# Shared expert of a routed feed-forward layer: units of 128 inner rows by 512 tokens in place of 256 by 256, and a down product in every unit

## What is computed

```python
x = x + xattn(layernorm(x), ctx, ...)          # 32 x 112 tokens of 256, 8 heads of 64
x = x + ffn(layernorm(x), ...)
# ffn, on n = layernorm(x), 3584 tokens:
out = routed(n)                                # 2 of 8 experts for each token, weighted
hs = (n @ Ws1) * silu(n @ Ws3)                 # shared expert: 256 -> 512 inner rows
out = out + hs @ Ws2                           # 512 -> 256
```

## Time and profile before

| what | value |
|---|---|
| median of 3 runs | 1096.32 us (1096.11 to 1097.06) |
| the profiled execution's own time | 1097.37 us |
| its span | 1095.3 us |
| mean granted TensorE clock | 0.985 of full |
| PE busy | 1061.2 us of the span |
| DVE busy | 743.3 us |
| ACT busy | 694.3 us |
| POOL busy | 705.3 us |

### The profile page before, as it was taken

One profiled execution on the slowest core, in us unless ns is written; L12 is line 12 of the kernel. 1 busy time (PEld: TensorE's weight loads), 2 busy tenths in 40 slices (PEclk: granted clock), 3 DMA queues, 4 the chain that ended last, 5 costly groups with the idle time before them and its releaser, 6 DMA issues. The chain is left out here.

```text
span 1095.3 us, 25507 instructions
## 1 busy us (share of the span) xinstructions
PE 1061.2 (97%) x7342; PEld 929.1 (85%) x7342; DVE 743.3 (68%) x1940; ACT 694.3 (63%) x1649; POOL 705.3 (64%) x658
## 2 busy tenths in 40 slices
PE   6999999999999999999999899999999999999996
PEld 4788888888888888888887799999888888888886
DVE  5788888888888888888888676656443333433332
ACT  6888888888888888888886554332334343343442
POOL 4988889888988888898887556555033223332233
PEclk9999999999999999999998999889999999999998
DMA  8014431442144214421532295223473354333861
GB/s 247 17 41 131 139 103 37 139 139 94 45 139 139 86 53 139 139 78 62 178 103 94 77 304 185 81 76 127 147 217 56 58 137 87 56 56 62 269 176 15
DMA packets 83985, 124.06 MB, mean 113 GB/s; under 512 B 7904, under 2 KB 48080, under 8 KB 83920
## 3 DMA queue, kind: packets, MB, share of 16 engines
q1 hardware_dynamic: 63664, 99.86, 28.0%
q0 software_dynamic: 11760, 15.15, 7.7%
q10 hardware_dynamic: 8496, 8.22, 2.6%
HBM read 74.44 MB, written 49.68 MB: 113 GB/s over the span
## 5 line engine op out<-in xcount | busy, mean ns | idle before, releaser
L559 POOL TENSOR_TENSOR probs<-probs,first_rows 112x750 f32<-112x750 f32 x128 | 184.0, 1438 | 66.1 <-DVE first_rows L1019 64.9
L1801 POOL DMA_INDIRECT out<-stage,to_row x48 | 74.9, 1560 | 175.7 <-ACT stage L1853 114.6
L2082 DVE TENSOR_TENSOR hT_lo<-banks,hT_hi 128x512 fp32r<-128x512 f32 x63 | 43.6, 692 | 185.3 <-ACT hT_hi L1845 179.4
L753 ACT ACTIVATE probs<-banks,first_rows 112x375 f32<-112x375 f32 x256 | 145.8, 573 | 18.2 <-DVE first_rows L1006 16.0
L1006 DVE TENSOR_REDUCE first_rows<-banks 112x2 f32<-112x750 f32 x128 | 119.6, 934 | 26.1 <-PE banks L1391 24.4
L519 POOL TENSOR_TENSOR v_both<-v_raw,v_both 125x512 fp32r<-125x512 f32 x96 | 123.7, 1288 | 7.5
L1012 DVE TENSOR_TENSOR pT<-banks,pT 125x672 fp32r<-125x672 f32 x128 | 108.8, 850 | 18.2 <-ACT pT L744 17.0
L1405 PEld LDWEIGHTS banks<-pT,v_both 125*128 125x128 f32 x768 | 99.7, 192 | 17.4 <-issue 10.4
L1405 PE MATMUL banks<-pT,v_both 125*128 125x224 f32 x768 | 110.9, 280 | 2.2 <-DVE oT_lo L1037 1.7
L515 POOL TENSOR_TENSOR v_both<-v_raw,one 125x512 fp32r<-125x512 f32 x96 | 110.6, 1152 | 0.1
L1417 PE MATMUL banks<-ident,probs 112*125 112x112 f32 x768 | 107.6, 277 | 1.4 <-POOL probs L559 0.7
(11 more groups left out here) (286 smaller groups left out, 3066.6 us busy)
## 6 DMA issues: line engine op xcount, KB each, us to landing
w_split_scratch<-stage SPq DMA_DIRECT2D x16, 1536.0 KB, 6.6
ring<-w_split_scratch SPq DMA_DIRECT2D x16, 1536.0 KB
stage<-in_L_ffn_W SPq DMA_DIRECT2D x48, 256.0 KB, 3.0
ctx_in<-in_ctx SPq DMA_DIRECT2D x32, 376.0 KB, 3.8
xg<-x_sorted_scratch ACTq DMA_DIRECT2D x59, 136.0 KB
x_in<-in_x SPq DMA_DIRECT2D x16, 224.0 KB, 3.3
x_res<-in_x SPq DMA_DIRECT2D x32, 112.0 KB, 2.1
x_scratch<-x SPq DMA_DIRECT2D x32, 112.0 KB, 1.9
```

The source lines that it names most:

```text
L559: pool.tensor_tensor(probs[:, two, :], probs[:, two, :], inv_sum[:, 2 * s:2 * s + 2].rearrange("p (e o) -> p e o", o=1).to_broadcast([N, 2 ...
L753: act.activation(probs[:, h % 4, :], S_BANKS[0:N, e, 0:M], ACT.Exp, bias=neg_max[:, h:h + 1], accum_out=row_sum[:, h:h + 1]).then_inc(exp_ ...
```

## The change

Chunk 0's two tiles stay as they were: two units of 256 inner rows by 256 tokens. Every later unit is 128 inner rows by the 512 tokens of a chunk, four units to a chunk, so that there are still 26 steps. `up_shared` then issues six products of 512 tokens where it issued twelve of 256. `down_shared(u)` now stands in every step, two units behind, between `up3` and `up1` instead of at the end of every second step: 12 products that add the unit's 128 inner rows to the sums of four tiles (`SUMS`). These sums stay open over four units, in four banks, two of which were the second banks of A3 and A1. So the shared units have one bank for each up product: `up3(g)` waits for `silu(g - 1)`, `up1(g)` for `hidden(g - 1)`. `add_y(c)` adds a chunk's four tiles at once, ahead of `hidden`, in the step in which the chunk's last down product is made.

```diff
+        SUMS = [A3[1], HT, A1[1], YB]
+        def parts_of(u):
+            if chunk_of(u) == 0:
+                return [(i, 2 * u + m, slice(m * PAIR + i * BLOCK, m * PAIR + (i + 1) * BLOCK))
+                        for i in range(2) for m in range(2)]
+            return [(i, (u - DONE_TILES) % MH, slice(i * BLOCK, (i + 1) * BLOCK)) for i in range(TC)]
+        def up_bank(g):
+            return g % 2 if g >= SHARED_FIRST else 0
...
-                act.activation(sil[g % 2], A3[g % 2][:], ACT.Silu).then_inc(sil_ready, 1)
+                act.activation(sil[g % 2], A3[up_bank(g)][:], ACT.Silu).then_inc(sil_ready, 1)
...
-                    wait(act, y_made, 2 * (g // 2))
+                    wait(act, y_made, g - 1)
...
-            def add_y(g):
-                t = STEPS[g][1]
-                if t < 2 * TC:
-                    dve.wait_ge(x1_loaded[t // TC], 16)
-                dve.wait_ge(y_made, g + 1)
-                dve.tensor_tensor(acc[:, t, :], acc[:, t, :], YS[g % 2], ALU.add).then_inc(y_added, 1)
+            def add_y(c):
+                if c < 2:
+                    dve.wait_ge(x1_loaded[c], 16)
+                dve.wait_ge(y_made, TC * (c + 1) - DONE_TILES)
+                for i, t in enumerate(tiles_of(c)):
+                    dve.tensor_tensor(acc[:, t, :], acc[:, t, :], sum_of(i), ALU.add).then_inc(y_added, 1)
...
-                if g % 2 and 3 <= g <= SHARED_FIRST + 1:
-                    add_y(g - 3)
-                    add_y(g - 2)
                 if 1 <= g <= LAST:
                     lo_of_hidden(g - 1)
+                if g == SHARED_FIRST:
+                    add_y(CHUNKS - 1)
+                elif 3 <= g < SHARED_FIRST and chunk_of(g - 1) > chunk_of(g - 2):
+                    add_y(chunk_of(g - 2))
                 if g < LAST:
                     hidden(g)
...
-                c, at = pair_of(u)
-                for mm in range(2):
+                c = chunk_of(u)
+                at = slice(0, CHUNK) if c else slice(DONE_TILES * BLOCK, CHUNK)
+                for mm, m in enumerate([(u - DONE_TILES) % MH] if c else [2 * u, 2 * u + 1]):
                     for k in range(2):
-                        base = 1024 - 1024 * first + k * H + (2 * (u % 2) + mm) * 128
+                        base = 1024 - 1024 * first + k * H + m * 128
...
-                        ps = o[:, mm * PAIR:(mm + 1) * PAIR]
+                        ps = o[:, 0:CHUNK] if c else o[:, mm * PAIR:(mm + 1) * PAIR]
...
-                wait(pe, sil_ready, g - 1)
+                wait(pe, sil_ready, g - 1 if g > SHARED_FIRST else g)
+                if g == SHARED_FIRST + 1:
+                    pe.wait_ge(y_added, SHARED_FIRST - 3)
...
-                wait(pe, hid_ready, g - 1)
+                wait(pe, hid_ready, g - 1 if g > SHARED_FIRST else g)
+                if g == SHARED_FIRST + 1:
+                    pe.wait_ge(y_added, SHARED_FIRST - 1)
...
+            def down_shared(u):
+                c = chunk_of(u)
+                pe.wait_ge(h_hi_ready, u + 1)
+                if c:
+                    pe.wait_ge(y_added, TC * c - DONE_TILES)
+                for i, m, at in parts_of(u):
+                    cols = slice(2048 + m * D, 2048 + (m + 1) * D)
                     for n, w in enumerate((w_hi1, w_lo1)):
+                        pe.matmul(sum_of(i), shT_hi[u % 2][:, at], w[:, cols], start=(m == 0 and n == 0), stop=False)
+                pe.wait_ge(h_ready, u + 1)
+                for i, m, at in parts_of(u):
+                    cols = slice(2048 + m * D, 2048 + (m + 1) * D)
+                    mm = pe.matmul(sum_of(i), shT_lo[u % 2][:, at], w_hi1[:, cols], start=False, stop=(m == MH - 1))
+                mm.then_inc(y_made, 1)
...
                 if g < LAST:
                     up3(g)
+                if 2 <= g <= SHARED_FIRST:
+                    down_shared(g - 2)
+                if g == SHARED_FIRST:
+                    down_shared(g - 1)
                 if g > SHARED_FIRST:
                     turn(g - 1)
...
-                if 2 <= g <= SHARED_FIRST and g % 2 == 0:
-                    down_shared(g // 2 - 1)
```

More of the change, by code:

```diff
@@ L1647, in experts, with chunk_of, tiles_of, sum_of @@
         PAIR = 2 * BLOCK
-        shT_hi, shT_lo = ([t[:].rearrange("p m n -> p (m n)").rearrange("p (m n) -> p m n", m=2) for t in ts]
-                          for ts in (hT_hi, hT_lo))
-        YS = [HT[:, 0:D], YB[:, 0:D]]
-        def pair_of(u):
-            t = DONE_TILES + 2 * (u // 2)
-            return t // TC, slice((t % TC) * BLOCK, (t % TC) * BLOCK + PAIR)
+        shT_hi, shT_lo = ([t[:].rearrange("p m n -> p (m n)") for t in ts] for ts in (hT_hi, hT_lo))
+        SUMS = [A3[1], HT, A1[1], YB]
+        def chunk_of(u):
+            return (u + DONE_TILES) // TC
+        def tiles_of(c):
+            return range(TC * c if c else DONE_TILES, TC * (c + 1))
+        def sum_of(i):
+            return SUMS[i][:, 0:D]
+        def parts_of(u):
[5 more added lines that the diff above has]
+            return g % 2 if g >= SHARED_FIRST else 0
         def shared_done(g):
@@ L1838, in hi_of_hidden @@
                     act.wait_ge(hid_ready, g + 1)
-                    wait(act, y_made, 2 * (g // 2))
-                    act.activation(shT_hi[g % 2], hid[g % 2][:].rearrange("p (m n) -> p m n", m=2),
-                                   ACT.Copy).then_inc(h_hi_ready, 1)
+                    wait(act, y_made, g - 1)
+                    act.activation(shT_hi[g % 2], hid[g % 2][:], ACT.Copy).then_inc(h_hi_ready, 1)
                     return
@@ L2077, in lo_of_hidden @@
                 if g < SHARED_FIRST:
-                    wait(dve, y_made, 2 * (g // 2))
-                    dve.tensor_tensor(shT_lo[g % 2], hid[g % 2][:].rearrange("p (m n) -> p m n", m=2),
-                                      shT_hi[g % 2].bitcast(F32), ALU.subtract).then_inc(h_ready, 1)
+                    wait(dve, y_made, g - 1)
+                    dve.tensor_tensor(shT_lo[g % 2], hid[g % 2][:], shT_hi[g % 2].bitcast(F32),
+                                      ALU.subtract).then_inc(h_ready, 1)
                     return
@@ L2208, in turn @@
                 if g == SHARED_FIRST:
-                    pe.wait_ge(y_added, SHARED_FIRST)
+                    pe.wait_ge(y_added, SHARED_FIRST - 2)
                 for m in range(MH):
@@ L2212, in turn @@
                 mm.then_inc(t_made, 1)
-            def down_shared(q):
-                pe.wait_ge(h_hi_ready, 2 * q + 2)
-                wait(pe, y_added, 2 * q)
-                cols = [slice(2048 + m * D, 2048 + (m + 1) * D) for m in range(MH)]
-                tiles = [slice(i * BLOCK, (i + 1) * BLOCK) for i in range(2)]
-                for i, at in enumerate(tiles):
-                    for n, w in enumerate((w_hi1, w_lo1)):
-                        for m in range(MH):
-                            pe.matmul(YS[i], shT_hi[m // 2][:, m % 2, at], w[:, cols[m]], start=(n == 0 and m == 0), stop=False)
-                pe.wait_ge(h_ready, 2 * q + 2)
-                for i, at in enumerate(tiles):
-                    for m in range(MH):
-                        mm = pe.matmul(YS[i], shT_lo[m // 2][:, m % 2, at], w_hi1[:, cols[m]], start=False,
-                                       stop=(m == MH - 1))
-                    mm.then_inc(y_made, 1)
+            def down_shared(u):
[5 more added lines that the diff above has]
+                    cols = slice(2048 + m * D, 2048 + (m + 1) * D)
+                    for n, w in enumerate((w_hi1, w_lo1)):
+                        pe.matmul(sum_of(i), shT_hi[u % 2][:, at], w[:, cols], start=(m == 0 and n == 0), stop=False)
[4 more added lines that the diff above has]
+                mm.then_inc(y_made, 1)
             def down(g):
```

10 lines of the change are left out of this document (5 added, 5 removed).

## The result

| | before | changed |
|---|---|---|
| median of 6 runs each | 1096.69 us (1092.88 to 1098.74) | 1092.28 us (1085.96 to 1096.38) |
| ratio | | 0.996, 95% interval 0.994 to 0.9979 |
| profiled execution, its span | 1097.37, 1095.3 us | 1092.94, 1090.8 us |
| from the first product of the first unit to step 27 (before: rows 5, from 629.03 to 782.13) | 153.10 us | 150.15 us |

The kernel is faster by 4.4 us, where I had forecast 9.1 (1087.2 us). The 4.43 us between the two profiled executions are 2.95 us in the stretch that the change touches, 1.29 us ahead of it, where the code is the same (the first unit starts at 627.74 in place of 629.03), and some 0.2 us behind it.

A forecast was written before the change was run, and what follows sets the result against it. PE was taken as the bound, busy 1061.2 of 1095.3 us; stream -1.2, idle time -5.3 and clock -2.6 sum to -9.1 us, giving 1088.3 against the profiled execution and 1087.2 as median, range 1079 to 1099.

The forecast's parts named there:

- The stream: Shared units' up products: 288 wide products replace 576 narrow ones, gain 1.7 us, taken as 1.2, bounds 0 and 3.
- Idle time, -5.3 us: PE in the shared units: the 6.3 us of idle time goes and 1.0 comes back; bounds -6.3 and 0.
- PE posts its signals late when it works through a long run of narrow products without a stop.: Shared units: inferred from signals 3.5 us late in step 9; the half-wide form should behave like the sorted stage.
- A: Rival: only the stream is won, late signals, router waits and clock losses stay; 1096.1 or 1093.6 us; chance 0.11.
- B: Rival: the single bank becomes the bound, up3 waits for a late silu; 1108 us, or 1100 if milder; chance 0.13.
- The place where it doesn't fit is step 22 to 24: Plan of the blocks on DVE delays hidden(23), so PE stands 0.9 us at up1(24), put down as 1.0.
- The clock, -2.6 us: Half-clock stretches in the shared units: three losses of 2.5 us, 7.6 in place of 10.2; bounds -10.2 and +10.2.
- three had a wait of 0.8 to 1.0 us ahead of them and all three lost the clock: Six routers: of the three without a wait one lost the clock; without waits three losses are counted.
- The single bank costs nothing: Shared units: up1 has 1.8 us to spare for hidden, up3 1.9 for silu, so no wait is expected.
- The gathered block costs nothing: First gathered block lands 7.8 us after hidden(22) starts; its transposes stand behind up1(24), at 9.1, so no wait.
- main case: Stream, idle time and clock all gain, with two to five clock losses: 1087.2 us, own range 1082 to 1093; chance 0.57.
- C: Rival: down products going round four banks cost the clock, 34 us more, 1121 us; chance 0.03.

The follow-up runs named there:

- h2: Kernel before with plain stores to fixed rows and the rank products behind the next up product: 1078.0 us, 0.9966 of the kernel before.
- h1: Changed kernel with plain stores to fixed rows and the rank products behind the next up product: 1078.74 us, 0.9966 of the kernel before.
- g1: Kernel before with plain stores to fixed rows in place of the indirect scatters: 1082.81 us, 0.9899 of the kernel before.
- g2: Changed kernel with plain stores to fixed rows in place of the indirect scatters: 1084.68 us, 0.9913 of the kernel before.
- e2: Changed kernel with each 512-wide up product issued as two of 256: 1095.06 us, 1.0 of the kernel before.
- f3: Changed kernel with each 512-wide up product issued as two of 256, run again in another set: 1093.53 us, 0.9972 of the kernel before.
- f1: Changed kernel unchanged, run again in another set: 1093.19 us, 0.9962 of the kernel before.
- f4: Changed kernel with plain stores to fixed rows in place of the indirect scatters, run again: 1084.17 us, 0.9882 of the kernel before.
- g1 to g4: Plain stores in four kernels: before, changed, changed with narrow products, changed with both moves; 1082.81, 1084.68, 1085.68, 1076.82 us.
- e7: Changed kernel with plain stores to fixed rows in place of the 56 indirect scatters: 1083.62 us, 1.0019 of the kernel before.
- e3: Changed kernel without the waits of PE that other waits cover: 1093.77 us, 0.9978 of the kernel before.
- e4: Changed kernel with the rank products moved from behind the router to behind the next up3: 1092.15 us, 0.9976 of the kernel before.
- f2: Changed kernel with plan one step earlier and rank products behind the next up product, run again: 1088.1 us, 0.9917 of the kernel before.
- e8: Kernel before with one bank for each up product instead of two, and the waits for it: 1082.18 us, 0.9996 of the kernel before.
- e5: Changed kernel with plan one step earlier and rank products behind the next up product: 1077.95 us, 0.9956 of the kernel before.
- g4: Changed kernel with plain stores, plan one step earlier and rank products behind the next up product: 1076.82 us, 0.9849 of the kernel before.
- both moves: Changed kernel with the plan one step earlier and the rank products behind the next up3: 1077.95 us in one set, 1088.1 us in another.
- set 3: Runs on one chip of the changed kernel, its both-moves, narrow and plain-store forms, beside the kernel before, which took 1096.43 us.

## Why the prediction was right or wrong

**The account of the stage** closes. The work at full clock is 135.6 us before (h2) and 133.4 after (h1). A half-clock stretch costs somewhat less than half its length: 6.8 us made g1 busy for 138.41 - 135.63 = 2.8 more, 17.0 us made g2 busy for 141.03 - 133.42 = 7.6 more, so 20.4 cost some 9, not 10.2. Before: 135.6 + 9 + 6.3 idle leaves 2.2 of 153.1; after: 133.4 + 9 + 6.7 leaves 1.1 of 150.15. The rest is what a stop of PE costs beyond its idle time. Set against g1, product by product, the first product behind a stop starts 0.16 us later than the idle time alone says, and the next one mostly another 0.1 us. The kernel before has eleven stops in the stage, the changed one five. So the 2.95 us come from the stream (2.2) and from six stops fewer (1.1), less 0.4 of idle.

1. **The stream: right, on the low side.** I took 1.2 with bounds 0 and 3, and 1.7 as the product; 2.2 is measured.
2. **Idle time, -5.3 us: wrong, measured +0.4.** Two steps failed.
   - *"PE posts its signals late when it works through a long run of narrow products without a stop."* The lateness comes beside the indirect scatters, in some sets of runs, at any width (e2, f3: 34 late signals; f1: 29; f4, g1 to g4: none). The sorted stage, which I took as the proof, has no scatters of token rows; that it also has wide products was a coincidence. I named it an inference and gave the cases in which signals stay late 0.11 (A) and 0.13 (B); that was too little for a cause read from two places that differ in more than one thing. The measured +0.4 lies outside the bounds of this term too: that waits of a new kind would come and the old ones stay was in neither bound.
   - *"The place where it doesn't fit is step 22 to 24"*: the place was right, the waiting instruction wrong. I priced `up1(24)` for `hidden(23)` at 1.0 us. I had seen the four adds behind the plan, but as something that delays `hidden`; the changed down product of unit 22 waits for these adds itself, in the same step, ahead of `up1(24)`. My own figures held that wait: the adds end 0.6 + 4.3 + 0.6 + 1.5 = 7.0 us after `hidden(22)` starts, and the down product could start one step less 0.3 us plus one `up3` after it, at 4.2 - 0.3 + 1.4 = 5.3, so 1.7 us. Measured are 1.6 in the profiles without late signals (e7, f4, g2, h1), and 2.9 with them (3.3 in e3 and f1, 2.3 in e4); those four have 3.4 us at half clock at its end as well.
3. **The clock, -2.6 us: wrong, measured 0.** The step was "three had a wait of 0.8 to 1.0 us ahead of them and all three lost the clock", from which I concluded that fewer waits mean fewer losses. g2 has no router wait and five losses; h1 and h2 have none with the 21 products of few columns split. The trigger behind the routers is in that run of products and not in the wait; a wait seems to add to it (f2 has the ranks apart and still 20.4 us at half clock, behind routers at 686.4 and 723.1 that waited 1.2 and 1.8 us, and at 664.8, whose neighbours had short stops). Why, with signals on time, the changed order loses the clock behind four or five routers (e7, f4, g2) and the order before behind two (g1) isn't settled. The price was sized too high as well: I took half of a stretch's length, 10.2 us for 20.4, where some 9 is what it costs. And one slice of 8 in the strip, at 575 to 602 us, lies in attention, where the clock falls with no router near it (587.8 us in the trace), in fourteen of the twenty profiles.
4. **The single bank costs nothing: right where signals are on time.** e8 has 0.9996 and one wait of 0.7 us. With late ones `up1(22)` waits for `hidden(21)`, 1.0 us in the first profile and 0.4 in f1.
5. **The gathered block costs nothing: right.** No wait for it is left in any profile of the changed kernel.

Of the rivals, A came closest (only the stream is won, late signals as before, the clock lost as often): it said 1093.6 to 1096.1, and 1092.28 was measured; its mechanism is what the profile shows. That 1092.28 also lies in the main case's own range, 1082 to 1093, is luck: two of the main case's three terms did not come. B did not come, not even with late signals: the longest wait for `hidden` in the changed kernel's two profiles is 1.0 us (2.0 in its narrow form, e2 and f3, at one step). C did not either: the down products go round four banks at every step, and the stage of e5 holds a clock of 1.00. The Trainium skill ("TensorE: Matmul & The Clock Gate", section "A second HAM failure mode: psum-queue depth-cycling") tells of a bf16 kernel with products of 512 columns whose TensorE, going round PSUM banks, is idle for short moments between its groups until the clock goes up and down; this case's trace doesn't show that. The sections ahead of and behind the stage did not change, as assumed; the 1.29 us ahead of it lie within the spread between executions, for the first unit starts between 625.8 and 630.6 us in the twenty profiles.

The forecast of "faster" held where signals come late, and would have failed where they don't. What the change won in the stage came from the stream and from fewer stops. By the profiles, late signals cost the old order more (a stage of 153.10 against 138.48 us in g1) than the new one (150.15 against 142.62 in g2, or 151.94 in f1 against 141.13 in f4), perhaps since a step of 4.2 us leaves the splits more time. That last is argued, not shown.

**The best version** is the changed kernel with both moves: 0.9917 (0.9892 to 0.9942) of the kernel before with late signals, 0.9956 (0.9941 to 0.9971) without. It beats the changed kernel by 5.1 us in set 3.

## What to carry to other kernels

Before counting idle time as a gain, find what causes it, with one kernel that takes the suspected cause away; an engine's late signals may belong to another engine's transfers, which the change leaves alone. When sums are kept over several units, the first unit of the next round waits for the whole tail of the last: look at what stands ahead of that tail in its engine's program, and move it away. Put an up product between two groups of products with few columns.

## What was not expected of the hardware

- Signals of PE come 1 to 5 us late beside GpSimd's indirect scatters of the token rows, several at a time: the products of 683.50, 684.05 and 684.49 were all signalled between 686.05 and 686.17, while PE went on with its products. With the same program it happens in some sets of runs and in others not, and it is worth 9 to 10 us of some 1095 within a set; the sets' medians of the kernel before differ by up to 15. Plain stores of the same bytes by the same engine don't bring it, and neither do the sparser indirect scatters of the sorted stage.
- Two groups of few columns, 16 products of 1.7 us and 5 of 0.5 us, in a row brought 3.4 us at half clock behind them in up to five of six places. The same groups with one up product between them (1.4 us; six products of 512 columns, in h2 twelve of 256) brought none, in five profiles of six (e4, e5, g4, h1, h2; not f2).
